# Attention scores of two heads at once, as 64-row fp32 products, in place of 128-row products of high and low parts

## The chip, the cores and the metric

The kernel runs on one core of one Trainium2 chip. The metric is the device time of one execution in microseconds (us); lower is better. The time before is 2332.83 us, the median of three runs (2322.44 to 2334.62).

## What is computed

The input is `[2, 2048, 256]` in fp32. A layer norm without gain is followed by causal attention with 16 heads of 64, a residual sum, a second layer norm, three blocks of quantised linear layers with GELU, and another residual sum. The part that matters here is the attention:

```python
keys    = einsum('bse,neh->bsnh', residual, W_key) + Bias_key       # S = 2048, 16 heads of 64
queries = einsum('bse,neh->bsnh', residual, W_query) + Bias_query
values  = einsum('bse,neh->bsnh', residual, W_values) + Bias_values
scores  = einsum('bknh,bqnh->bnqk', keys, queries) / sqrt(64)
scores  = where(q_idx < k_idx, 1e-10, scores)     # masked scores are 1e-10, not minus infinity
probs   = softmax(scores, axis=3)
weighted = einsum('bnqk,bknh->bqnh', probs, values)
```

A masked key still has a weight in the softmax, so the kernel adds a masked part to each numerator and denominator, and it needs the true maximum of each row before the exponentials.

## The kernel before, in words

Heads are worked on in pairs: 8 pairs per batch and 2 batches make N = 16 pairs. The 2048 queries of a pair are 4 groups of 512 columns, and its keys are 16 blocks of 128. `tiles_of` (line 38) cuts a group into tiles of two key blocks; there are NT = 20 tiles for each pair, in groups 3, 2, 1, 0. That makes 40 blocks per pair; 16 of them lie on the diagonal and have 512, 384, 256 or 128 columns, and the other 24 have 512.

TensorE's order is written out by hand (lines 932 to 945). While it works on tile t of pair i, it issues the score products of tile t+1 (`scores`, line 848), then the products with the values for tile t (`weighted`, line 869). Between them stand small pieces of the next pair's work, each at a slot number of a table, six slots to a tile: 12 projections (`project`, line 738, slots 0, 3, ..., 33), 40 pairs of bf16 products for the row maxima (`max_unit`, line 793, always at odd slots, table `MAX_AT`), transposes and denominators (`FIN`). ScalarE and VectorE follow the same tables.

The scores are done in TensorE's fast fp32r format, which is not exact to fp32. So every query and key is split in two. ScalarE writes the high part (`high`, line 955), VectorE writes what is left, the low part (`low`, line 1103), and both go to a tensor in device memory, `high_and_low` (`keep_split`, line 414). From there `install` (line 422) loads them as stacks of 128 rows: `kk` holds the key's high part twice, `qq` the query's high over its low part, `kl` the key's low part over a row of ones, `qm` the query's high part over the negated row maximum. One block of one head is then two products of 128 rows, L859 and L861, plus a bf16 product with `never_above` on the diagonal (L864). For two heads that is four products, and two more on the diagonal.

PSUM has 8 banks: 3 for scores (`SCORE_BANKS`), 4 that all background pieces take in turn (`BANKS`), and 1 for the outputs. A background piece waits in `bank_read` until the piece that had its bank BANKS places earlier has been read: a projection of queries or keys by VectorE's low part (`proj_read`), a max product by VectorE's maximum (`take_max`, L1118 or L1121).

The output side of a product with the probabilities uses 64 columns of the array for each head, so the two heads of L880 are two column tiles. The two heads of L798 are two row tiles of 64 rows each. All other products use the whole array.

Of the kernel before, what the change touches and what calls it, by code (L numbers as in the profile page):

```python
# [7 lines left out]
F32 = mybir.dt.float32  # L8
# [109 lines left out]
BANKS = 4  # L118
# [4 lines left out]
SCORE_BANKS = 3  # L123
# [12 lines left out]
def half_index(i, t, h, half):  # L136

    return NHALF * i + HALVES_TO[t] + len(halves_of(t)) * h + half
# [15 lines left out]
def background(n_pairs_in_all, n_pairs):  # L154
# [23 lines left out]
    counts = {"proj": 0, "max": 0, "fin": 0, "den": 0, "ln": len(PROJ_CHUNKS), "lora": 0, "weight": 0}  # L178
    for use in order:
        kind = {"vt": "fin", "mt": "fin"}.get(use[0], use[0])  # L180
        first[use] = len(users)
        for _ in range(2 if kind in ("max", "ln") else 1):
            counts[kind] += 1
            users.append((kind, counts[kind]))
# [8 lines left out]
def attention(nc, x, w_qkv, b_qkv, ffn_weights, parts, max_kept, kept, inverses, ot, home):  # L193
# [14 lines left out]
    with ExitStack() as ctx:  # L208
# [5 lines left out]
        def sem(name):  # L214
# [5 lines left out]
        never_above = sb("never_above", [P, P], BF16)  # L220
# [9 lines left out]
        split = [sb(f"split{b}", [P, 4, CH], F32R) for b in range(2)]  # L230
# [17 lines left out]
        qq = sb("qq", [P, 2, S], F32R)  # L248
        qm = sb("qm", [P, 2, S], F32R)
        kk = sb("kk", [P, 2, S], F32R)  # L250
        kl = sb("kl", [P, 2, S], F32R)
# [15 lines left out]
        w_q = ([split[0][:, l].bitcast(I32).rearrange("p (h d) -> p h d", h=halves) for l in range(4)]  # L267
               + [split[1][:, l].bitcast(I32).rearrange("p (h d) -> p h d", h=halves) for l in range(2)])
        w_unit = [t.bitcast(F32) for t in w_q]
        la_in = [xs[0:R, 3, l // 2, (l % 2) * D:(l % 2 + 1) * D] for l in range(4)]  # L270
        la_in += [split[1][0:R, 2, l * D:(l + 1) * D].bitcast(F32) for l in range(2)]
        lbt = [split[1][0:R, 3, l * D:(l + 1) * D].bitcast(F32) for l in range(2)]
# [17 lines left out]
        kl_zeroed = sem("kl_zeroed")  # L290
# [18 lines left out]
        proj_read = sem("proj_read")  # L309
# [4 lines left out]
        split_kept = [sem(f"split_kept{b}") for b in range(2)]  # L314
        stack_in = [sem(f"stack_in{c}") for c in range(4)]
# [59 lines left out]
        with nc.Block() as block:  # L375

            @block.sync
            def _(sp):
                def load_weights(j):

                    sp.wait_ge(proj_read, START + NPROJ * j)
# [15 lines left out]
                def load_ffn_weights():  # L397

                    sp.wait_ge(proj_done, START + NPROJ * N)
                    sp.wait_ge(bf_ready, START + 8 * N)  # L400
                    for b in range(2):
                        sp.wait_ge(split_kept[b], START + 64 * N)
                    for b, of in enumerate((slice(0, 4), slice(4, n_layers))):
                        n_of = of.stop - of.start
                        sp.dma_start(split[b][:, 0:n_of].bitcast(I32).rearrange("p l (h d) -> p (l h) d", h=halves),
# [3 lines left out]
                    sp.dma_start(split[1][0:R, 2].bitcast(F32).rearrange("r (l d) -> r l d", d=D),  # L409
# [3 lines left out]

                def keep_split(j, c):

                    k = PROJ_CHUNKS.index(c)
                    sp.wait_ge(proj_read, START + NPROJ * j + 3 * k + 2)
                    for h in range(2):
                        sp.dma_start(parts[j % 2, c].rearrange("z p h t -> h p z t")[h],
                                     split[k % 2][64 * h:64 * h + 64, :, :].bitcast(F32)).then_inc(split_kept[k % 2], 16)  # L420

                def install(j, c):

                    k = PROJ_CHUNKS.index(c)
                    sp.wait_ge(split_kept[k % 2], START + 64 * j + 32 * (k // 2 + 1))
                    of = parts[j % 2, c]
                    for dst, src in ((qq[:, :, cols(c)], of[0:2].rearrange("z p h t -> (z p) h t")),
                                     (kk[0:64, :, cols(c)], of[2]), (kk[64:128, :, cols(c)], of[2]),
                                     (qm[0:64, :, cols(c)], of[0]), (kl[0:64, :, cols(c)], of[3])):
                        sp.dma_start(dst.bitcast(F32), src).then_inc(stack_in[c], 16)  # L430
# [6 lines left out]
                def install_max(j, c):  # L437

                    sp.wait_ge(row_kept, START + 16 * (nth(j, c) + 1))
                    sp.dma_start(qm[64:65, :, cols(c)].bitcast(F32),  # L440
                                 max_kept[j % 2, c].rearrange("(o h r) t -> o h (r t)", o=1, h=2)).then_inc(row_in[c], 16)

                def install_chunk(j, c):

                    sp.wait_ge(pv_done, START + NT * (j - 1) + LAST_TILE[c] + 1)
                    install(j, c)
# [65 lines left out]
                for c in PROJ_CHUNKS:  # L512
                    keep_split(0, c)
                sp.wait_ge(consts, START + 1)
                load_weights(1)
                for c in GROUPS:
                    install(0, c)
# [5 lines left out]
                for i in range(N):  # L523
                    more = i + 1 < N
                    if i:
                        spread_inverse(i - 1, 1)
                        install_chunk(i, 0)
                        take_den(i - 1, 0)
                        install_max(i, 0)
                    if more:  # L530
                        keep_split(i + 1, 3)
                    if i:
# [6 lines left out]
                    if more:  # L539
                        keep_split(i + 1, 2)  # L540
                    spread_masked(i, 2)
                    if more:
                        keep_split(i + 1, 1)
# [1192 lines left out]
```

## Time and profile before

| | us |
|---|---|
| median of the runs before | 2332.83 |
| profiled execution, its own time | 2334.97 |
| span of its core | 2333.2 |
| TensorE busy | 2228.3 (96%) |
| VectorE busy | 1328.3 (57%) |
| ScalarE busy | 910.7 (39%) |
| GpSimd busy | 1350.7 (58%) |
| mean granted TensorE clock | 0.98 of full speed |

The attention fills the span up to about 2040 us; its first 94 us prepare the first pair. The feed-forward part follows. Every fp32 matmul appears as two records of TensorE, a product in fp32r or bf16 as one. An end of a matmul is modelled in the profile, so the time from one start to the next says more than the duration.

### The profile page before, as it was taken

Reading aid. Unit: us, or ns where it says so; the run is one execution under the profiler, and the core shown is the slowest. Engines: PE = TensorE matmul, PEld = TensorE weight load, DVE = VectorE, ACT = ScalarE, POOL = GpSimd, SP = SyncE. Lnnn points to the kernel's source line nnn. Section 1 sums busy time; section 2 is a strip of 40 time slices with the busy share of each in tenths; the row PEclk is TensorE's granted clock in tenths of the full one; section 3 lists DMA queues with packets and bytes.
Section 4 is the critical chain, followed back from the end, with each engine's and each line's share of the span. In section 5 each row is a group of like instructions: output and inputs, shape, how many; then the busy total and the mean of one; then the engine's idle time right before and its main releaser. Section 6 shows DMA issues by size and latency. Waiting matters only on the chain. (4 is left out here: it accounts for less than half of the span.)

```text
span 2333.2 us, 31181 instructions
## 1 busy us (share of the span) xinstructions
PE 2228.3 (96%) x10080; PEld 1133.2 (49%) x10080; DVE 1328.3 (57%) x3583; ACT 910.7 (39%) x1764; POOL 1350.7 (58%) x1211
## 2 busy tenths in 40 slices
PE   6899999999999999999999999999999998899987
PEld 2344444444444445444444444444444445777764
DVE  6755555555555566555656565555555563466664
ACT  2244444444444446444444444444444442110110
POOL 2277777777777777777677776767777611211110
PEclk9699999999999999999999999999999998999998
DMA  4644445454445463535363636363627323411100
GB/s 110 144 98 123 122 115 130 118 126 119 126 112 132 114 166 104 141 96 148 84 160 93 152 87 157 79 163 77 169 76 184 89 78 110 166 68 46 64 18 18
DMA packets 206272, 261.33 MB, mean 112 GB/s; under 512 B 74720, under 2 KB 91296, under 8 KB 206112
## 3 DMA queue, kind: packets, MB, share of 16 engines
q1 hardware_dynamic: 206112, 259.35, 42.2%
q8 instruction: 82, 1.34, 0.3%
q14 instruction: 78, 0.64, 0.1%
HBM read 169.87 MB, written 88.87 MB: 111 GB/s over the span
## 5 line engine op out<-in xcount | busy, mean ns | idle before, releaser
L711 POOL TENSOR_TENSOR acc<-acc,probs 128x512 f32<-128x512 f32 (+1 forms) x900 | 996.5, 1140 | 286.6 <-ACT probs L1056 286.4
L1056 ACT ACTIVATE probs<-ps_s 128x512 f32<-128x512 f32 (+1 forms) x1152 | 603.6, 576 | 740.1 <-PE ps_s L861 456.3
L1121 DVE TENSOR_REDUCE partial<-ps_bg 128x1 f32<-128x512 f32 x768 | 489.6, 684 | 201.2 <-PE ps_bg L798 200.2
L859 PE MATMUL ps_s<-qq,kk 128*128 128x512 f32 (+3 forms) x1280 | 579.5, 453 | 8.0 <-ACT probs L1056 4.9
L880 PE MATMUL ps_o<-probs,v 128*64 128x512 f32 (+3 forms) x2560 | 541.2, 543 | 1.8 <-DVE num L1145 1.8
L861 PE MATMUL ps_s<-qm,kl 128*128 128x512 f32 (+3 forms) x1280 | 469.4, 367 | 0.0
L746 PE MATMUL ps_bg<-home,w_in 128*128 128x512 f32 x768 | 368.6, 603 | 12.6 <-DVE split L1103 10.3
L859 PEld LDWEIGHTS ps_s<-qq,kk 128*128 128x128 f32 x1280 | 244.0, 191 | 202.2 <-issue 140.8
L798 PE MATMUL ps_bg<-k_bf,q_bf 64*128 64x512 bf16 (+3 forms) x1280 | 252.8, 363 | 21.2 <-DVE split L1103 14.0
L880 PEld LDWEIGHTS ps_o<-probs,v 128*64 128x64 f32 x2560 | 155.7, 136 | 233.4 <-issue 185.7
L861 PEld LDWEIGHTS ps_s<-qm,kl 128*128 128x128 f32 x1280 | 243.4, 190 | 37.4 <-issue 21.5
L1118 DVE CUSTOM_DVE_ANT_0 junk<-ps_bg,mask_q 128x512 bf16<-128x512 f32 (+3 forms) x512 | 229.0, 484 | 57.1 <-issue 55.1
L798 PEld LDWEIGHTS ps_bg<-k_bf,q_bf 64*128 64x128 bf16 x1280 | 67.2, 93 | 345.7 <-issue 283.4
L1103 DVE SCALAR_TENSOR_TENSOR split<-ps_bg,bias,split 128x512 fp32r<-128x512 f32 x128 | 94.3, 736 | 211.0 <-ACT q_bf L967 126.3
L746 PEld LDWEIGHTS ps_bg<-home,w_in 128*128 128x128 f32 x768 | 141.1, 191 | 119.9 <-issue 96.8
L1450 POOL TENSOR_TENSOR c_rstd<-c_var,c_minus_half 128x4 f32<-128x4 f32 x32 | 35.3, 1104 | 275.0 <-DVE c_var L1625 275.0
L704 POOL TENSOR_TENSOR acc<-probs 128x512 f32<-128x512 f32 x90 | 112.9, 1277 | 114.6 <-ACT probs L1056 67.3
L675 POOL TENSOR_TENSOR num<-num,scale 128x512 f32<-128x512 f32 x64 | 89.8, 1403 | 129.9 <-DMA scale<-inverse_sums 129.9
L964 ACT ACTIVATE split<-ps_bg,bias 128x512 fp32r<-128x512 f32 x128 | 88.0, 688 | 163.0 <-PE ps_bg L746 163.0
L1160 DVE RECIPROCAL inverse<-den_sq 32x32 f32<-32x32 f32 x64 | 21.5, 337 | 212.0 <-DMA den_sq<-den_rows 212.0
L667 POOL TENSOR_TENSOR masked_num<-v_from,e 128x512 f32<-128x512 f32 x64 | 76.9, 1201 | 89.7 <-DVE num L1145 88.5
L1598 ACT ACTIVATE c_yt<-c_ps,c_be,c_ga 128x512 f32<-128x512 f32 x48 | 33.7, 776 | 238.0 <-PE c_ps L1495 238.0
(114 smaller groups left out, 1886.4 us busy)
## 6 DMA issues: line engine op xcount, KB each, us to landing
high_and_low<-split SPq DMA_DIRECT2D x128, 512.0 KB, 5.9
qq<-high_and_low SPq DMA_DIRECT2D x64, 512.0 KB, 4.4
kk<-high_and_low SPq DMA_DIRECT2D x128, 256.0 KB, 5.3
qm<-high_and_low SPq DMA_DIRECT2D x64, 256.0 KB, 6.0
kl<-high_and_low SPq DMA_DIRECT2D x64, 256.0 KB, 6.3
e<-masked_weights SPq DMA_DIRECT2D x128, 128.0 KB, 3.0
scale<-inverse_sums SPq DMA_DIRECT2D x128, 128.0 KB, 2.9
heads_turned<-num SPq DMA_DIRECT2D x64, 256.0 KB, 3.3
```

The source lines that it names most:

```text
L675: g.tensor_tensor(num[:, n % NUMS, :], num[:, n % NUMS, :], scale[:, group % 2, :], ALU.mult).then_inc(o_ready, 1)
L704: g.tensor_tensor(acc[h][:, group % 2, :], pr[:, 0:CH], pr[:, CH:2 * CH], ALU.add).then_inc(added, 1)
L711: g.tensor_tensor(acc[h][:, group % 2, q0:q0 + w], acc[h][:, group % 2, q0:q0 + w], probs[h][:, probs_slot(i, t), at:at + w], ALU.add).the ...
L746: mm = pe.matmul(bank("proj", j, u), w_in[:, s, m, :], xs[:, c, s, :], start=(s == 0), stop=(s == halves - 1))
L798: pe.matmul(bank("max", j, n, h)[:, 0:w], q_bf[HEAD[h], qb * P:(qb + 1) * P], k_bf[HEAD[h], CH * u:CH * u + w], start=True, stop=True).the ...
L859: pe.matmul(out, kk[:, h, kb * P:(kb + 1) * P], qq[:, h, q], start=True, stop=False, skip_group_check=True)
L861: mm = pe.matmul(out, kl[:, h, kb * P:(kb + 1) * P], qm[:, h, q], start=False, stop=not diagonal, skip_group_check=True)
L880: mm = pe.matmul(ps_o[64 * h:64 * h + 64, q0:q0 + w], v[:, kb, 64 * h:64 * h + 64], probs[h][:, probs_slot(i, t), at:at + w], start=first, ...
L1056: nc.scalar.activation(probs[h][:, probs_slot(i, t), CH * half:end], ps_s[:, k % SCORE_BANKS, 0:end - CH * half], ACT.Exp, scale=SCORE_SCA ...
L1103: e.scalar_tensor_tensor(part[:, 2 * m + 1, :], bank("proj", j, u), bias[:, m:m + 1], part[:, 2 * m, :].bitcast(F32), ALU.add, ALU.subtrac ...
L1118: e.tensor_tensor_reduce(junk[:, k, 0:w], of, mask_q[:, CH - w:CH], 1.0, 3 * NEVER, ALU.add, ALU.max, to).then_inc(max_read, 1)
L1121: e.reduce_max(to, of, AX.X).then_inc(max_read, 1)
```

## The change

Queries and keys stay whole. ScalarE writes them in fp32 to `q_all` and `k_all`, both double-buffered by pair. One block of one head is one true fp32 product of 64 rows; the two heads lie in the upper and lower half of the array. A second product, of 64 rows in fp32r, adds the negated maximum of the row (`max_rows`, times one row of ones in `max_gate`). On the diagonal two bf16 products of 64 columns per head add the mask. VectorE's low part, the trips through `high_and_low` and the installs are gone; the row maximum is installed by two DMAs instead of one. A tile's four score calls become two, each for both heads, and the pieces that stood between them stand two by two. The scores get 4 banks and the background gets 3. A projection's bank is now free once ScalarE has read it.

```diff
-BANKS = 4
+BANKS = 3
-SCORE_BANKS = 3
+SCORE_BANKS = 4
...
-                    nc.scalar.activation(split[k % 2][:, 2 * m, :], bank("proj", j, u), ACT.Identity,
+                    exact = (q_all, k_all)[m]
+                    nc.scalar.activation(exact[:, j % 2, cols(c)], bank("proj", j, u), ACT.Identity,
...
-                    dve.wait_ge(hi_ready, START + 8 * j + 2 * (u // 3) + m + 1)
-                    dve.wait_ge(bf_ready, START + 8 * j + 2 * (u // 3) + m + 1)
-                    part = split[u // 3 % 2]
-                    e.scalar_tensor_tensor(part[:, 2 * m + 1, :], bank("proj", j, u), bias[:, m:m + 1],
-                                           part[:, 2 * m, :].bitcast(F32), ALU.add, ALU.subtract
-                                           ).then_inc(proj_read, 1)
...
-                    pe.matmul(out, kk[:, h, kb * P:(kb + 1) * P], qq[:, h, q], start=True, stop=False,
-                              skip_group_check=True)
-                    mm = pe.matmul(out, kl[:, h, kb * P:(kb + 1) * P], qm[:, h, q], start=False,
-                                   stop=not diagonal, skip_group_check=True)
+                    out = []
+                    for h in range(2):
+                        k = half_index(i, t, h, at // CH)
+                        if n == blocks[0] and k >= SCORE_BANKS:
+                            pe.wait_ge(p_ready, START + k - SCORE_BANKS + 1)
+                        out.append(ps_s[:, k % SCORE_BANKS, at % CH:at % CH + w])
+                        pe.matmul(out[h], k_all[HEAD[h], i % 2, kb * P:(kb + 1) * P], q_all[HEAD[h], i % 2, q],
+                                  start=True, stop=False, skip_group_check=True)
+                    last = [pe.matmul(out[h], max_gate[HEAD[h], :], max_rows[HEAD[h], q], start=False,
+                                      stop=not diagonal, skip_group_check=True) for h in range(2)]
                     if diagonal:
-                        mm = pe.matmul(bank_s[:, at % CH:at % CH + P], ident_bf[:, :], never_above[:, :], start=False,
-                                       stop=True, skip_group_check=True)
+                        for part in range(2):
+                            last = [pe.matmul(out[h][:, 64 * part:64 * part + 64], never_later[HEAD[h], h, part, :],
+                                              ident_bf[HEAD[h], 64 * h:64 * h + 64], start=False, stop=(part == 1),
+                                              skip_group_check=True) for h in range(2)]
...
-                        for h in range(2):
+                        if ni < N:
+                            scores_wait(ni, nt)
+                        for n in range(2):
                             if ni < N:
-                                scores_wait(ni, nt, h)
-                            for n in range(2):
-                                if ni < N:
-                                    scores(ni, nt, h, n)
-                                between(i, 6 * t + 2 * h + n)
+                                scores(ni, nt, n)
+                            between(i, 6 * t + 2 * n)
+                            between(i, 6 * t + 2 * n + 1)
```

## Rows read from the trace of the kernel before

**Rows 1.** Page, part 1: busy time, share of the span, instructions.
```profile
PE 2228.3 (96%) x10080; PEld 1133.2 (49%) x10080; DVE 1328.3 (57%) x3583; ACT 910.7 (39%) x1764; POOL 1350.7 (58%) x1211
```
**Rows 2.** Windows: stretch, length, busy time (instructions) by engine, clock, DMA share, GB/s.
```profile
0.00:94.00 94.00, 63.92 (x179) 22.97 (x180) 72.17 (x228) 20.04 (x35) 13.76 (x22) 0.81 0.59 143
236.00:1900.00 1664.00, 1634.49 (x7544) 760.32 (x7543) 947.44 (x2566) 756.61 (x1492) 1176.57 (x1054) 1.00 0.48 122
```
**Rows 3.** Waits of TensorE, whole span: total us, times, longest.
```profile
PE ps_bg L798 <- DVE split L1103: 14.0, 15, 0.9
PE ps_bg L746 <- DVE split L1103: 10.3, 8, 1.9
...
PE ps_s L859 <- ACT probs L1056: 4.9, 1, 4.9
```
**Rows 4.** Groups by form, TensorE: line, shapes, count, busy us, mean ns, idle before.
```profile
L859 PE MATMUL ps_s<-qq,kk 128*128 128x512 f32 x896 | 428.1, 478 | 8.0 <-ACT probs L1056 4.9 <-DMA qm<-maxima 3.1
...
L864 PE MATMUL ps_s<-never_above,ident_bf 128*128 128x128 bf16 x512 | 117.6, 230 | 0.0
```
**Rows 5.** Timeline, TensorE, 614.4 to 618.4 us: start, duration, instruction, records.
```profile
614.41 0.40 PE L861 MATMUL ps_s<-qm,kl 128*128 128x512 f32 x1
...
614.74 0.39 PE L798 MATMUL ps_bg<-k_bf,q_bf 64*128 64x512 bf16 x2
...
615.06 0.50 PE L859 MATMUL ps_s<-qq,kk 128*128 128x512 f32 x1
...
615.40 0.40 PE L861 MATMUL ps_s<-qm,kl 128*128 128x512 f32 x1
...
615.64 0.40 PE L859 MATMUL ps_s<-qq,kk 128*128 128x512 f32 x1
...
615.88 0.40 PE L861 MATMUL ps_s<-qm,kl 128*128 128x512 f32 x1
...
616.21 0.39 PE L798 MATMUL ps_bg<-k_bf,q_bf 64*128 64x512 bf16 x2
...
616.52 1.94 PE L880 MATMUL ps_o<-probs,v 128*64 128x512 f32 x8
...
618.39 0.39 PE L798 MATMUL ps_bg<-k_bf,q_bf 64*128 64x512 bf16 x2
```
**Rows 6.** Timeline, TensorE, 609.3 to 611.1 us: a projection and what follows.
```profile
609.29 1.88 PE L746 MATMUL ps_bg<-home,w_in 128*128 128x512 f32 x4
...
611.10 0.39 PE L798 MATMUL ps_bg<-k_bf,q_bf 64*128 64x512 bf16 x2
```
**Rows 7.** Timeline, TensorE, 646.0 to 646.4 us: a diagonal block of 256 columns.
```profile
645.97 0.39 PE L859 MATMUL ps_s<-qq,kk 128*128 128x256 f32 x1
646.19 0.28 PE L861 MATMUL ps_s<-qm,kl 128*128 128x256 f32 x1
646.31 0.23 PE L864 MATMUL ps_s<-never_above,ident_bf 128*128 128x128 bf16 x1
646.35 0.31 PE L859 MATMUL ps_s<-qq,kk 128*128 128x128 f32 x1
```
**Rows 8.** Groups of VectorE from 236 to 1900 us, columns as in rows 4.
```profile
L1121 DVE TENSOR_REDUCE partial<-ps_bg 128x1 f32<-128x512 f32 x672 | 429.6, 685 | 187.0 <-PE ps_bg L798 186.1
...
L1134 DVE TENSOR_TENSOR_SCAN v_from<-ones_row,v_from,vt 128x512 f32<-128x512 bf16 x56 | 86.8, 1550 | 1.5
L1103 DVE SCALAR_TENSOR_TENSOR split<-ps_bg,bias,split 128x512 fp32r<-128x512 f32 x109 | 80.1, 735 | 172.2 <-ACT q_bf L967 99.9 <-ACT k_bf L967 72.1
L1097 DVE TENSOR_SCALAR vt<-ps_bg,bias 128x512 f32<-128x512 f32 x55 | 41.3, 751 | 39.2 <-PE ps_bg L746 39.2
L1152 DVE TENSOR_TENSOR den_rows<-ps_bg,den_rows 65x512 f32<-65x512 f32 x56 | 38.4, 686 | 60.2 <-PE ps_bg L825 30.6 <-DMA den_rows<-masked_den 29.5
```
**Rows 9.** Timeline, all engines, 91.7 to 93.7 us: the end of the preparation.
```profile
91.70 0.67 SPq L440 DMA_DIRECT2D qm<-maxima  x1
...
93.68 0.77 PE L859 MATMUL ps_s<-qq,kk 128*128 128x512 f32 x1 [3.08 <-DMA qm<-maxima]
```

More of the change, by code:

```diff
@@ L136, in half_index @@
 def half_index(i, t, h, half):
-    return NHALF * i + HALVES_TO[t] + len(halves_of(t)) * h + half
+    return NHALF * i + HALVES_TO[t] + 2 * half + h
 def tile_end(i, t):
@@ L190, with attention @@
 NFIRST = len(FIN_FIRST)
-def attention(nc, x, w_qkv, b_qkv, ffn_weights, parts, max_kept, kept, inverses, ot, home):
+def attention(nc, x, w_qkv, b_qkv, ffn_weights, max_kept, kept, inverses, ot, home):
     n_chunks, _, _, D = x.shape
@@ L229, in attention @@
         xs = home.rearrange("p (c s t) -> p c s t", c=4, s=halves)
-        split = [sb(f"split{b}", [P, 4, CH], F32R) for b in range(2)]
+        staged = [sb(f"staged{b}", [P, 4, CH]) for b in range(2)]
         vt = sb("vt", [P, S])
@@ L556, in _ @@
                     masked_rows(i, 3)
-                    if more:
-                        install_chunk(i + 1, 3)
                     take_den(i, 3)
@@ L621, in _ @@
                 g.memset(minus_half[:, :], -0.5).then_inc(zeroed, 1)
-                for tile in (ident, ident_bf, never_above, mask_q):
+                for tile in (ident, ident_bf, mask_q):
                     g.memset(tile[:, :], 0.0).then_inc(zeroed, 1)
+                g.memset(never_later[:, :, :, :], 0.0).then_inc(zeroed, 1)
                 pool.wait_ge(zeroed, START + 5)
@@ L650, in _ @@
                 pool.wait_ge(set_up, START + 1)
-                g.memset(kl[64:65, :, :].bitcast(F32), 1.0).then_inc(consts, 1)
+                for h in range(2):
+                    g.memset(max_gate[64 * h:64 * h + 1, :].bitcast(F32), 1.0).then_inc(consts, 1)
                 def masked_denominators(i):
@@ L925, in _ @@
                             turn_values(0, c)
-                pe.wait_ge(consts, START + 1)
-                for h in range(2):
-                    scores_wait(0, 0, h)
-                    for n in range(2):
-                        scores(0, 0, h, n)
+                pe.wait_ge(consts, START + 2)
+                scores_wait(0, 0)
+                for n in range(2):
+                    scores(0, 0, n)
                 turn_max(0, 0)
@@ L1033, in _, with exponentials @@
                         high(0, n)
-                act.wait_ge(consts, START + 1)
+                act.wait_ge(consts, START + 2)
                 for k, (kind, c) in enumerate(FIN_FIRST[:-1]):
                     evacuate(0, kind, c, k + 1)
-                def exponentials(i, t, h, n):
+                def exponentials(i, t, n):
                     tile = TILES[t][1]
-                    if h == 0 and n == 0:
+                    half = tile[n][3] // CH
+                    if n != halves_of(t)[half][-1]:
+                        return
+                    if half == 0:
                         user = NT * i + t - NP_SLOTS
@@ L1049, in exponentials @@
                                 act.wait_ge(fin_written, START + fin_before(i, 0))
-                    half = tile[n][3] // CH
-                    if n != halves_of(t)[half][-1]:
-                        return
-                    k = half_index(i, t, h, half)
                     end = tile[n][3] + tile[n][2]
-                    act.wait_ge(s_ready, START + k + 1)
-                    nc.scalar.activation(probs[h][:, probs_slot(i, t), CH * half:end],
-                                         ps_s[:, k % SCORE_BANKS, 0:end - CH * half], ACT.Exp,
-                                         scale=SCORE_SCALE).then_inc(p_ready, 1)
-                for h in range(2):
-                    for n in range(2):
-                        exponentials(0, 0, h, n)
+                    for h in range(2):
+                        k = half_index(i, t, h, half)
+                        act.wait_ge(s_ready, START + k + 1)
+                        nc.scalar.activation(probs[h][:, probs_slot(i, t), CH * half:end],
+                                             ps_s[:, k % SCORE_BANKS, 0:end - CH * half], ACT.Exp,
+                                             scale=SCORE_SCALE).then_inc(p_ready, 1)
+                for n in range(2):
+                    exponentials(0, 0, n)
                 evacuate(0, "mt", 0, NFIRST)
@@ L1066, in _ @@
                         t = n // 6 + 1
[L1067 to L1070 removed]
+                        if n % 6 in (0, 2) and t < NT:
+                            exponentials(i, t, n % 6 // 2)
+                        elif n % 6 in (0, 2) and i + 1 < N:
+                            exponentials(i + 1, 0, n % 6 // 2)
                         for u in range(NPROJ):
```

139 lines of the change are left out of this document (45 added, 94 removed).

## The prediction

> **What bounds the kernel now.** I read the busy times first. TensorE is busy for 96% of the span, every other engine for under 60% [rows 1]. The windows then say where: from 236 to 1900 us, which is nearly all of the attention, TensorE is busy 1634.49 of 1664 us at full clock, while GpSimd, the next, has 1176.57 and ScalarE 756.61 [rows 2]. The list of its waits confirms that it is hardly ever held up: 14.0 and 10.3 us for VectorE's low parts, 4.9 us for an exponential [rows 3]. So in the attention the time is the length of TensorE's own list, and what another engine saves is worth nothing unless TensorE waited for it. Only the first 94 us differ: there VectorE is busy for 72.17 us, TensorE for 63.92 with its clock at 0.81 [rows 2]. The feed-forward part isn't touched.
>
> Durations of matmuls overlap, so I price them by the distance from one start to the next. Two fp32r products of 512 columns start 0.24 us apart (615.40, 615.64, 615.88) [rows 5]. An fp32 product on the whole array costs 0.86: two of them take from 609.29 to 611.10, 1.81 us, about 0.10 of which is the change to what follows [rows 6]. Four fp32 products on column tiles of 64 take from 616.52 to 618.39, 1.87 us for two pairs [rows 5]: less such a change 0.86 to 0.90 a pair, so the two heads overlap fully.
>
> **The change part by part.**
>
> *A, blocks off the diagonal.* There are 896 products of 512 columns at L859, and 512 products on the diagonal, a quarter of which are 512 wide [rows 4]: 896 - 128 = 768, or 384 blocks of two heads. Before, such a block is four fp32r products, 4 x 0.24 = 0.94 us (they are 0.233 to 0.24 apart). After, it is one row pair in fp32 and one row pair in fp32r. No row shows an fp32 row pair. From below it can't be quicker than one fp32 product, 0.86; from above it is two of them, 1.72. I take 0.86, since the fp32 column pair [rows 5] and the bf16 row pair (0.32 with its change, both heads together) both overlap. The fp32r pair is 0.24, at most 0.48. So 0.86 + 0.24 = 1.10 against 0.94: +0.16 x 384 = **+61 us**.
>
> *B, the 256 diagonal blocks.* One head's block of 256 columns costs 0.38 us, from 645.97 to 646.35 [rows 7], two heads 0.76. After: the fp32 pair 0.43 (half of 0.86), the fp32r pair 0.12 to 0.24, and two pairs of masks of 64 columns. Their price is not shown; the nearest row is the mask of 128 columns before, 0.04 to its successor (646.31 to 646.35) [rows 7], so 0.08 to 0.20 for both pairs. The sum is 0.63 to 0.87, -0.13 to +0.11 per block, and as a 512-wide block gains A's 0.16 on top, up to +0.3. I take +0.02: **+5 us**, with -33 and +77 as its ends.
>
> *C, changes between array layouts.* A max pair stands in the 64-row layout. 614.41 to 614.74 is 0.33 where 0.24 is normal; the pair itself takes 0.32; the first score product after it 0.34 [rows 5]. Entering, leaving and starting again cost some 0.10 each. I counted the order by the slot tables. Before, a pair of heads has 93 changes of layout, 27 of them into a score product, which pays twice: 93 x 0.10 + 27 x 0.10 = 12.0 us. After, scores and maxima share the layout, so the 22 changes from a max pair to a score and 18 back are gone, but projections and transposes, which shared the scores' layout, now need them: 82 changes, 11 into scores, 9.3 us, plus 17 starts of projections and transposes at 0 to 0.10, say 0.05: 10.2. The difference is 1.8 to 2.0 us in each of 15 pairs: **-30 us**; ends 0 and -90 (below).
> The Trainium skill ("TensorEngine Tiling (Array Packing)", Key Properties) says that changing the tiling mode drains TensorE, while changing the tile does not. The trace agrees: the extra 0.09 to 0.10 stands at the changes alone. By a reading of it in which only the 40 changes at maxima counted, C would be -60 us; by its letter the new ones at projections count as well, which is what I took.
>
> *D, waits that go.* The low parts held TensorE for 14.0 + 10.3 us [rows 3]. They are gone and the bank of a projection is free after ScalarE, which the low part waited for anyway: **-24 us**, ends -24 and -10.
>
> *E, three background banks instead of four.* This is the added wait. The second product of a max pair now takes the bank of the first product of the max pair before it, which must have been read; behind it on TensorE's queue stand all further scores and value products. That read ends about 0.39 + 0.68 + 0.10 = 1.2 us after its product starts (0.39 [rows 5], 0.685 [rows 8]; 0.10 for two handovers is my allowance). Where the value products lie between, max pairs are 2.2 us apart (616.21 to 618.39), with 1.0 to spare; where scores lie between they were 1.47 apart (614.74 to 616.21) [rows 5] and will be 0.22 + 1.10 = 1.3. The slack is 0.1 us. What VectorE does besides then comes out: 4 scans, 4 value projections and 4 denominators per pair, 4 x (1.55 + 0.75 + 0.69) = 12.0 us [rows 8]. 22 of 40 max pairs are followed by a score, so 6.6 us per pair could show, 99 us in all; 0 is the other end. The nearest row is the wait that a bank more left: 24 us, all behind low parts of 0.735 us, 8 per pair [rows 3, 8]. I take **+25 us**.
>
> *F, the first 94 us.* VectorE loses 8 low parts of 0.735, 5.9 us [rows 8], and the first score no longer waits 3.08 us for its row of maxima [rows 9], which was queued behind the installs. TensorE's last maxima are late next, and they follow VectorE: **-7 us**, ends 0 and -12.
>
> *At nothing:* 512 fewer transfers: TensorE waited for a DMA once in the attention [rows 9]. ScalarE's two passes over each projection stay. The order of exponentials changes, but ScalarE has 756.61 of 1664 us [rows 2] and four score banks in place of three. GpSimd's sums are unchanged. The second DMA for each row of maxima is behind a full tile of work.
>
> Sum: 61 + 5 - 30 - 24 + 25 - 7 = +30 us. The profiled execution took 2334.97 us, so 2365; it is 2.1 above the median of the runs, so I predict **2363 us**, with its own range from 2335 to 2400.
>
> **The rivals.**
> 1. *It cancels.* VectorE keeps ahead, E is 0: 2338 us. For it: it waits 187.0 us for maxima before L1121 [rows 8], so it is early on the whole. Against: the short distances above. Chance 0.15.
> 2. *Faster: the layout changes decide.* At 22 x 0.20 + 18 x 0.09 = 6.0 us per pair, 90 us in all go, if the new changes at projections cost nothing because the two row tiles run out one after the other while the next weights load; E is 5. 61 + 5 - 90 - 24 + 5 - 7 = -50: 2283 us. It decides once the saving passes 60 us, 4 us per pair. Against: projection to max pair costs the change just the same (609.29 to 611.10) [rows 6]. Chance 0.10.
> 3. *VectorE becomes the bound through the banks.* E is 99: 2437 us. Chance 0.10.
> 4. *The fp32r row pair does not hide.* It streams 0.24 us, in which weights for both heads must come in, now four times per block instead of two; one after the other it is 0.48: 0.24 x 384 + 0.12 x 256 = +123: 2486 us. Weight loads are 0.11 us each on the mean (1133.2 over 10080) [rows 1], which two at once just fit. Chance 0.05.
> The Trainium skill ("TensorE: Matmul & The Clock Gate", LDWEIGHTS) says that a load's time goes by its columns and not by its rows, so a 64-row load is as long as a 128-row one. That speaks for this rival; no 64-row fp32 load is in this trace.
> 5. *The fp32 row pair does not overlap at all.* +0.86 x 384 + 0.43 x 256 = +440: about 2800 us. Against it stand both kinds of pair in rows 5. Chance 0.03.
>
> **How the numbers follow.** The forecast has 0.57. Within 0.5% means 2321 to 2344 us, about what a measurement of this kernel can tell from no change. Faster: rival 2 and an edge of the forecast, 0.12. Same: rival 1 and the forecast's lower edge, 0.21. Slower: the rest, 0.67. The range is 2318 to 2440: it leaves out rival 2, rivals 4 and 5.
>
> **What the profile of the changed kernel would show.** A: starts of the fp32 row products 0.43 us apart with both heads at one time, a 512-wide block 1.10 us in all; 1.3 or more refutes it. B: diagonal blocks of 256 at 0.63 to 0.87. C: max pair to score 0.22, and 0.10 extra around each projection. D: no wait of TensorE behind a projection of queries or keys. E: TensorE's waits for L1118, L1121, L1134 or L1152 add up to 25 us, most of them where scores stand between max pairs. F: the first score at about 87 us instead of 93.68. The prediction is wrong if the clock of the attention falls below 1.00, if row pairs don't overlap, or if E is far from 25.

## The result, and the profile of the changed kernel

The changed kernel takes 2340.87 us in the median of 15 runs, the kernel before 2327.24 in as many (its first three, known at the forecast, had 2332.83). The ratio on record is 1.0075, with an interval from 1.0061 to 1.0088: slower by 14 to 20 us; the two medians alone are 13.6 us apart. One of the 15 runs of the changed kernel, 2586.83 us at a granted clock of 0.842, is left out of the ratio. The way was forecast, the size was not: 2363 us, 30 us above the median known then. Of the 22 us between 2363 and 2340.87, some 6 come from that median, which the later runs lowered, and 16 from the change itself.

The first view is the page of the changed kernel: busy times, and what the DMA queues moved.

```profile
PE 2251.2 (96%) x11872; PEld 1024.5 (44%) x11872; DVE 1233.5 (53%) x3455; ACT 904.0 (39%) x1764; POOL 1346.7 (58%) x1212
...
DMA packets 117192, 93.71 MB, mean 40 GB/s; under 512 B 67552, under 2 KB 84128, under 8 KB 117024
```

TensorE is still the bound and 23 us busier than in [rows 1]. VectorE has lost 95 us of work, and the DMAs have shrunk from 261.33 MB to 93.71. The windows (columns as in [rows 2]) show the attention at full clock, and TensorE idle for 16 us of 1664, where it was 29.5:

```profile
236.00:1900.00 1664.00, 1647.87 (x9106) 661.38 (x9102) 866.41 (x2452) 749.09 (x1488) 1178.56 (x1054) 1.00 0.12 34
```

Next, TensorE's timeline in the changed kernel: start, duration, instruction, records. A max pair, a block, another block, a max pair, the value products:

```profile
622.29 0.39 PE L759 MATMUL ps_bg<-k_bf,q_bf 64*128 64x512 bf16 x2
622.52 1.02 PE L817 MATMUL ps_s<-q_all,k_all 64*128 64x512 f32 x4
622.97 0.80 PE L819 MATMUL ps_s<-max_rows,max_gate 64*128 64x512 f32 x2
623.61 1.02 PE L817 MATMUL ps_s<-q_all,k_all 64*128 64x512 f32 x4
624.06 0.79 PE L819 MATMUL ps_s<-max_rows,max_gate 64*128 64x512 f32 x2
624.70 0.39 PE L759 MATMUL ps_bg<-k_bf,q_bf 64*128 64x512 bf16 x2
625.02 1.94 PE L841 MATMUL ps_o<-probs,v 128*64 128x512 f32 x8
```

Block to block is 1.09 us (622.52 to 623.61). The four records of the two fp32 heads all start within 0.43 us; the two that belong together start 3 to 4 ns apart, so both heads take 0.86 us and the maximum's pair the other 0.23. A max pair before a score costs 0.23 (622.29 to 622.52) where it cost 0.32 in [rows 5]; before the value products it still costs 0.32.

Spans alone say little here, so the comparison goes pair by pair. I took the start of the first value product of each pair of heads, and the distance to the next pair's. "Last pair" is from its first value product to its last, "rest" what comes behind:

```
                        first value   15 distances      clean pair   last pair   rest
                        product       together
before                  104.48        1759.94           116.1         79.2       389.6
changed                 101.71        1773.59           118.0         73.0       390.8
difference               -2.8          +13.7             +1.9          -6.2       +1.2   = +5.9
```

A clean pair is the commonest distance. In the changed kernel twelve of 15 pairs take 117.98 to 118.06 us; the others are 119.0, 124.1 (the one with the second batch's layer norm) and 114.1 (the last distance). In the kernel before only four take 116.1; nine are uneven, 116.3 to 119.8, the one with the layer norm takes 120.3 and the last 114.6. So the clean pair grew by 1.9 us, 29 us in all, and 15 us of unevenness and 6 us of the last pair went. (The two profiled executions are 5.9 us apart and the medians 13.6, since the profiled one of before, 2334.97, is 7.7 above its median. That the unevenness differs from run to run would explain this; it isn't shown, since one execution of each kernel is profiled.)

Where the last pair of before lost its time stands in four views of that kernel: the timelines of VectorE, the DMA queue, ScalarE and TensorE.

```profile
1879.91 0.34 DVE L1160 RECIPROCAL inverse<-den_sq 32x32 f32<-32x32 f32 x1 [8.41 <-DMA den_sq<-den_rows]
```
```profile
1869.17 0.57 SPq L430 DMA_DIRECT2D qq<-high_and_low  x1
1869.78 1.26 SPq L430 DMA_DIRECT2D kk<-high_and_low  x2
1871.08 0.60 SPq L430 DMA_DIRECT2D qm<-high_and_low  x1
1871.72 0.60 SPq L430 DMA_DIRECT2D kl<-high_and_low  x1
1872.45 1.21 SPq L483 DMA_DIRECT2D den_sq<-den_rows  x2
```
```profile
1882.42 1.58 ACT L1056 ACTIVATE probs<-ps_s 128x512 f32<-128x512 f32 x3 [5.96 <-DVE acc L1191]
```
```profile
1883.07 0.79 PE L859 MATMUL ps_s<-qq,kk 128*128 128x512 f32 x1 [4.90 <-ACT probs L1056]
1883.66 0.63 PE L861 MATMUL ps_s<-qm,kl 128*128 128x512 f32 x1
1884.22 3.68 PE L880 MATMUL ps_o<-probs,v 128*64 128x512 f32 x8
1887.83 0.53 PE L859 MATMUL ps_s<-qq,kk 128*128 128x512 f32 x1
```

The sums of the denominators, a tiny transfer, are issued behind the five installs of chunk 0, and VectorE goes on 7.4 us after that (1872.45 to 1879.91). VectorE stands in its reciprocal for 8.41 us; in the last pair it also adds the probabilities, so ScalarE waits 5.96 us for VectorE, and TensorE 4.90 us for ScalarE. Then TensorE works at the lower level of its clock (1.2 GHz) until 1887.9: value products that take 1.94 elsewhere take 3.68. The same lower level stands in two other pairs of that trace, for 3.41 us from 1410.1 and from 1529.5, behind waits of 1.75 and 1.90 us for a low part at L746; they are the two longest of the uneven ones, 119.65 and 119.79 us.

TensorE's waits in the changed kernel, the whole span (the feed-forward part's left out):

```profile
PE ps_bg L759 <- ACT k_bf L924: 7.3, 15, 0.5
...
PE ps_bg L759 <- DVE den_rows L1102: 4.2, 14, 1.2
PE ps_bg L707 <- ACT k_bf L924: 3.2, 3, 1.1
...
PE ps_bg L759 <- DVE partial L1068: 2.4, 6, 1.0
PE ps_bg L759 <- DVE partial L1071: 1.5, 5, 0.3
```

With six smaller ones these are 24.5 us, all for a background bank. This isn't to be set against the 24.3 for low parts in [rows 3] alone: the kernel before waited about 8 us more for such banks, of which these are the larger two:

```profile
PE ps_bg L798 <- DVE partial L1118: 3.6, 9, 1.6
...
PE ps_bg L798 <- DVE partial L1121: 1.6, 5, 0.4
```

### The profile page after: what moved, and what is told of

The parts are those of the page before. It is cut to its first block and busy times, and to the rows that moved or that the text cites. A ratio compares the mean times of both kernels' runs of the same rounds, so it can differ in the third digit from the quotient of the medians.

```text
span 2339.1 us, 33962 instructions
## 1 busy us (share of the span) xinstructions
PE 2251.2 (96%) x11872; PEld 1024.5 (44%) x11872; DVE 1233.5 (53%) x3455; ACT 904.0 (39%) x1764; POOL 1346.7 (58%) x1212
## 2 busy tenths in 40 slices
DMA packets 117192, 93.71 MB, mean 40 GB/s; under 512 B 67552, under 2 KB 84128, under 8 KB 117024
## 5 line engine op out<-in xcount | busy, mean ns | idle before, releaser
L1014 ACT ACTIVATE probs<-ps_s 128x512 f32<-128x512 f32 (+1 forms) x1152 | 588.6, 572 | 754.3 <-PE ps_s L819 491.8
L817 PE MATMUL ps_s<-q_all,k_all 64*128 64x512 f32 (+3 forms) x2560 | 609.7, 549 | 0.0
L819 PE MATMUL ps_s<-max_rows,max_gate 64*128 64x512 f32 (+3 forms) x1280 | 453.5, 696 | 0.0
L707 PE MATMUL ps_bg<-home,w_in 128*128 128x512 f32 x768 | 381.8, 620 | 6.9 <-ACT k_bf L924 3.2
L759 PE MATMUL ps_bg<-k_bf,q_bf 64*128 64x512 bf16 (+3 forms) x1280 | 269.3, 361 | 19.7 <-ACT k_bf L924 7.3
L817 PEld LDWEIGHTS ps_s<-q_all,k_all 64*128 64x128 f32 x2560 | 223.7, 188 | 126.8 <-ACT probs L1014 66.9
L1055 DVE TENSOR_SCALAR vt<-ps_bg,bias 128x512 f32<-128x512 f32 x64 | 48.1, 751 | 305.0 <-PE ps_bg L707 305.0
L819 PEld LDWEIGHTS ps_s<-max_rows,max_gate 64*128 64x128 f32 x1280 | 128.3, 187 | 114.8 <-issue 104.9
L628 POOL TENSOR_TENSOR masked_num<-v_from,e 128x512 f32<-128x512 f32 x64 | 76.1, 1190 | 89.6 <-DVE num L1095 88.3
L1102 DVE TENSOR_TENSOR den_rows<-ps_bg,den_rows 65x512 f32<-65x512 f32 x64 | 44.0, 687 | 94.7 <-PE ps_bg L786 45.9
L1469 PE MATMUL c_ps<-c_yt,home 128*128 128x512 f32 x192 | 86.8, 605 | 4.9 <-ACT c_yt L1548 4.9
```

The costliest lines, as they stand in the source:

```text
L707: mm = pe.matmul(bank("proj", j, u), w_in[:, s, m, :], xs[:, c, s, :], start=(s == 0), stop=(s == halves - 1))
L759: pe.matmul(bank("max", j, n, h)[:, 0:w], q_bf[HEAD[h], qb * P:(qb + 1) * P], k_bf[HEAD[h], CH * u:CH * u + w], start=True, stop=True).the ...
L817: pe.matmul(out[h], k_all[HEAD[h], i % 2, kb * P:(kb + 1) * P], q_all[HEAD[h], i % 2, q], start=True, stop=False, skip_group_check=True)
L819: last = [pe.matmul(out[h], max_gate[HEAD[h], :], max_rows[HEAD[h], q], start=False, stop=not diagonal, skip_group_check=True) for h in ra ...
L1014: nc.scalar.activation(probs[h][:, probs_slot(i, t), CH * half:end], ps_s[:, k % SCORE_BANKS, 0:end - CH * half], ACT.Exp, scale=SCORE_SCA ...
L1469: mm = pe.matmul(ps[L][:, s, :], w[:, 2 * k + 1, r, s * P:(s + 1) * P], yt[L][:, r, :], start=(r == 0), stop=(r == halves - 1))
```

## The experiments

Each ran on one chip beside the kernel before; ratios are against that. All diffs are against the kernel named first.

**1. The projections moved (changed kernel).**
```diff
-PROJ_SLOT = [3 * u for u in range(NPROJ)]
+PROJ_SLOT = [6 * (u // 2) + 3 + 2 * (u % 2) for u in range(NPROJ)]
+MAX_AT = [n - 1 if n % 6 == 3 else n for n in MAX_AT]
```


> The changed kernel with the next pair's projections at slots 3 and 5 of each six (beside the value products) instead of 0 and 3, and the max pairs of slot 3 one slot earlier. Theory (each change between array layouts costs about 0.10 us, and 0.10 more where fp32 or fp32r work starts): 66 changes per pair of heads instead of 82, and 5 fewer starts of scores after a projection, so about 2.1 us less in each of 15 pairs, 32 us less than the changed kernel, ratio to the kernel before about 0.992. Rival (the layout changes cost nothing, the clean pair of 118.0 us is longer for another reason): same time as the changed kernel, ratio 1.0075. Second rival (moved work collides with the three background banks): slower than 1.0075.

Measured: 2315.17 us, 0.9962 (0.9949 to 0.9976). Its clean pair takes 116.3 us instead of 118.0, its 15 distances 1748.84 us: 24.8 less. A clean pair gives 0.08 us for each of the 21 changes and starts, near the 0.10 of the theory, and both rivals are out. This kernel already beats both.

**2. The same move in the kernel before.**
```diff
-PROJ_SLOT = [3 * u for u in range(NPROJ)]
+PROJ_SLOT = [6 * (u // 2) + 3 + 2 * (u % 2) for u in range(NPROJ)]
```


> The kernel before with the projections at slots 3 and 5, nothing else. Here projections share the scores' layout, so the move buys nothing: 98 changes instead of 93, 5 x 0.10 x 15 = 8 us slower, ratio 1.003. If moving projections helped for a reason that has nothing to do with layouts (banks, ScalarE's order), this kernel would gain as well: 0.99.

Measured: 2347.21 us, 1.0106 (1.0088 to 1.0125). There it costs 25 us, three times what was expected; so experiment 1's gain is not one of moving as such. The clean pair is 116.8 us instead of 116.1, where the theory's five more changes were to cost 0.5. The rest is unevenness: TensorE waits 14.2 us for VectorE's value projection in that kernel, a wait that the original didn't show.

**3. Scores in fp32r (changed kernel).** The edit gives `q_all` and `k_all` the type fp32r.
```diff
-        q_all = sb("q_all", [P, 2, S])
-        k_all = sb("k_all", [P, 2, S])
+        q_all = sb("q_all", [P, 2, S], F32R)
+        k_all = sb("k_all", [P, 2, S], F32R)
```


> The changed kernel with the 64-row score product in fp32r instead of fp32 (the scores lose the exactness of fp32). Theory (A): a pair of 512 columns costs 0.24 instead of 0.86 us, so 384 x 0.62 = 238 us and on the 256 diagonal blocks about 0.3 each, 77 us: 315 us less if TensorE stays the bound, about 2026 us, ratio 0.870. Rival (ScalarE, GpSimd or VectorE takes over at once): GpSimd is busy 1346.7 us of 1180 to 1900 in the attention; it would hold the time at about 2150 us or more, ratio 0.92.

Measured: 2244.42 us, 0.9661 (0.9643 to 0.9679): a third of the 315 us. TensorE's waits say why (236 to 1900 us):

```profile
PE ps_bg L759 <- DVE partial L1068: 104.8, 44, 7.0
PE ps_bg L759 <- DVE partial L1071: 10.0, 29, 0.4
```

GpSimd, the rival's bound, is busy for 1185.21 of these 1664 us and isn't it. With quick scores TensorE is held by VectorE, and a clean pair is 112.5 us, with 10.7 us of idle TensorE where the changed kernel had 1.0. Most of that is one stop, which comes back in nearly every pair. Here it is in VectorE's and TensorE's timelines:

```profile
621.62 8.79 DVE L1084 TENSOR_TENSOR_SCAN v_from<-ones_row,v_from,vt 128x512 f32<-128x512 bf16 x1
```
```profile
630.81 0.28 PE L759 MATMUL ps_bg<-k_bf,q_bf 64*128 64x128 bf16 x1 [6.93 <-DVE partial L1068]
```

One scan of VectorE takes 8.79 us, 14 times in this run; in the changed kernel 47 of 64 take 1.3 us and none over 2.2. The maxima behind it are late, TensorE stops for 6.9 us, and its granted clock is at the lower level (1.2 GHz) for 10.24 us, from 626.6 to 636.8, so the 6 us of work behind the stop go at half speed. Why the scan is so long there no run shows. The last pair, which has no such stop, is 17.4 us shorter (55.6 against 73.0), close to the 315 / 16 = 19.7 us of the theory. So the fp32 price is real, but most of it is lost again to this stop and the slow clock behind it.

**4. Four background and three score banks (changed kernel).**
```diff
-BANKS = 3
+BANKS = 4
-SCORE_BANKS = 4
+SCORE_BANKS = 3
```


> The changed kernel with four background banks and three score banks, as before the change. Theory (E): the fourth bank takes back TensorE's waits in the attention for a background bank, 11.7 us for ScalarE and 11.6 us for VectorE in the list of waits, and three score banks cost nothing: 20 us less, ratio 0.999. Rival: both heads' scores are issued together, so with three score banks the second block must wait for an exponential of the first: more than 1.0075.

Measured: 2447.74 us, 1.0536 (1.0517 to 1.0555). The rival was right. The clean pair is 125.1 us. The waits of TensorE's weight loads in the window 236 to 1900 us, first of this kernel, then of the changed one, show 75 us more of waiting for an exponential:

```profile
PEld ps_s L817 <- ACT probs L1014: 129.8, 199, 0.8
```
```profile
PEld ps_s L817 <- ACT probs L1014: 54.8, 73, 0.8
```

One thing got faster: with four background banks the first score starts at 81.07 us, in the changed kernel at 89.67.

**5. The kernel before without installs from pair 1 on.** `install_chunk` keeps its wait and issues nothing; the score products wait for pair 0's installs alone.
```diff
-                    install(j, c)
...
-                            pe.wait_ge(stack_in[c], START + 80 * (i + 1))
+                            pe.wait_ge(stack_in[c], START + 80)
```


> The kernel before with the install DMAs of pairs 1 to 15 left out (their scores use pair 0's queries and keys; the row maxima are still installed). Theory (transfers cost time where a denominator's small transfer is queued behind an install): in the last pair VectorE waited 8.41 us for den_sq, TensorE then 4.90 us for an exponential and went on at half clock; that stall goes, 9 us less, and the uneven pairs (116.1 to 120 us each) get closer to 116.1: ratio 0.992 to 0.996. Rival (installs are hidden, as the prediction had it at nothing): 1.000, and a last pair of 79 us as before.

Measured: 2310.68 us, 0.9936 (0.9922 to 0.9950). Thirteen of the 15 distances are 116.1 to 116.3 us, and the last pair takes 71.9 instead of 79.2. The installs were not hidden. In its trace the pairs are 25 us shorter together, though the first value product comes 4.6 us later.

**6. The sums ahead of the installs (kernel before).** Two lines change places; all work stays.
```diff
-                        install_chunk(i, 0)
                         take_den(i - 1, 0)
+                        install_chunk(i, 0)
```


> The kernel before with one line moved: the denominators' transfer of the last group is issued ahead of the installs of chunk 0 instead of behind them. Nothing is left out. Theory: the last pair takes about 71 to 73 us instead of 79.18, the rest stays: 7 us less, ratio 0.997. Rival (the 7.4 us of the small transfer are not due to the installs ahead of it): 1.000.

Measured: 2311.10 us, 0.9940 (0.9925 to 0.9954), twice the expected gain. The last pair is 71.9 us and the clean ones are 116.1, as if the installs weren't there: the rival is out. VectorE's waits, first before, then here:

```profile
DVE inverse L1160 <- DMA den_sq<-den_rows: 212.0, 31, 8.8
```
```profile
DVE inverse L1160 <- DMA den_sq<-den_rows: 102.8, 22, 7.4
```

TensorE's list of waits no longer has the 10.3 us at L746 of [rows 3] nor the 4.9 for an exponential; the other wait for low parts is the same to the digit:

```profile
PE ps_bg L798 <- DVE split L1103: 14.0, 15, 0.9
```

So 10.3 of the 24.3 us "for low parts" were the installs' doing. The trace is 24.6 us shorter in its pairs (17.3 in the 15 distances, 7.3 in the last), the median 14 us. VectorE still waits 102.8 us for sums, but TensorE isn't held up by that.

**7. A short low part (kernel before).** From pair 1 on it has 8 columns.
```diff
-                    e.scalar_tensor_tensor(part[:, 2 * m + 1, :], bank("proj", j, u), bias[:, m:m + 1],
+                    lw = slice(0, CH if j == 0 else 8)
+                    e.scalar_tensor_tensor(part[:, 2 * m + 1, lw], bank("proj", j, u)[:, lw], bias[:, m:m + 1],
...
```


> The kernel before with VectorE's low part of 8 columns instead of 512 from pair 1 on (the rest of the low parts is left as it was, so the scores of those pairs are wrong in their low bits); its waits for ScalarE stay. Theory (D): TensorE's 24 us of waits for low parts shrink by the 0.7 us that each takes: 15 us less, ratio 0.993. Rival (VectorE's length does not matter, only its wait for ScalarE): 1.000.

Measured: 2311.48 us, 0.9937 (0.9921 to 0.9954). Its profiled execution took 7710.27 us, so its trace isn't read. The gain is as expected, but 6 gives as much, so it doesn't say by itself whether both are one stall.

**8. Both (6 and 7).**

> before_sums_first with the low part of 8 columns from pair 1 on (low bits of the scores are left as they were). Theory (with the installs out of the way the low parts hold TensorE only 0.9 us in each pair): another 0.9 x 15 = 13 us less at most, ratio 0.989. Rival (both earlier gains of 14 us were the same stall, and a VectorE that is on time hides its low parts): 0.994 again.

Measured: 2301.05 us, 0.9889 (0.9874 to 0.9905): 0.5% below experiment 6, 10 to 12 us. They are two things. The trace shows less than the times: a clean pair is 115.5 us instead of 116.1, and TensorE's wait at L798 falls from 14.0 to 6.1 us. So the low part costs TensorE some 0.6 us per pair even when VectorE is on time.

**9. The changed kernel's order, in the kernel before.** The loops over heads and blocks change places in `scores` and `exponentials`, `half_index` becomes `2 * half + h`, and the background pieces stand two by two.
```diff
-    return NHALF * i + HALVES_TO[t] + len(halves_of(t)) * h + half
+    return NHALF * i + HALVES_TO[t] + 2 * half + h
...
-                        for h in range(2):
+                        if ni < N:
+                            scores_wait(ni, nt, 0)
+                        for n in range(2):
...
-                            for n in range(2):
-                                if ni < N:
+                                for h in range(2):
...
+                            between(i, 6 * t + 2 * n)
+                            between(i, 6 * t + 2 * n + 1)
```


> The kernel before with the block order of the changed kernel: both heads of a block together, exponentials likewise, background pieces two by two; the products, layouts and banks stay. Theory (order alone costs nothing, the 2 us per pair come from products and layouts): 1.000. Rival (issuing both heads together needs the fourth score bank, as 107 us for taking it away from the changed kernel suggest): up to 100 us more, ratio 1.02 to 1.045.

Measured: 2315.06 us, 0.9957 (0.9941 to 0.9972). Neither theory: the order gains 10 us, and its last pair is still 78.2 us long, so this isn't the installs' stall. The clean pair is 115.6 instead of 116.1; by the slot tables the order has 90 changes of layout instead of 93 and 24 starts of scores instead of 27, six items for 0.5 us. And three score banks are enough here, so the 107 us of 4 come with the order only when the fp32 products are in it.

**10. Order and sums first together (kernel before).**

> The kernel before with the block order of the changed kernel and the denominators' transfer ahead of the installs. If the two add up (115.6 us for a clean pair, 71.9 for the last): 8 us less than before_sums_first, about 2303 us, ratio 0.991. Rival (the order's gain of 0.0043 was the same waits for low parts): 0.994.

Measured: 2304.69 us, 0.9893 (0.9872 to 0.9914). They add up: the clean pair is 115.6 us and the last 71.3.

**11. Three background and four score banks (kernel before).**
```diff
-BANKS = 4
+BANKS = 3
...
-SCORE_BANKS = 3
+SCORE_BANKS = 4
```


> The kernel before with three background banks and four score banks. Theory (E as forecast, the low part is read last): TensorE waits for VectorE's low parts and maxima through the missing bank, some 25 to 60 us more, ratio 1.01 to 1.025. Rival (the score banks are worth more than the background bank, as in the changed kernel, where the fourth score bank was worth 107 us): under 1.00.

Measured: 2392.47 us, 1.0269 (1.0243 to 1.0294), just above the expected range:

```profile
PE ps_bg L746 <- DVE split L1103: 36.3, 19, 3.2
...
PE ps_bg L798 <- DVE split L1103: 20.1, 15, 1.3
```

The waits for low parts are 56.4 us where they were 24.3, a further 10 us are lost before the first value product, and TensorE's clock is at the lower level in seven places for 3.41 us each. A low part that is read last lives badly with three banks; ScalarE's reading does better (24.5 us of waits in all in the changed kernel). Each kernel is slower with the other's bank counts.

**12. The masks left out (changed kernel).**
```diff
-                    diagonal = kb // 4 == group
+                    diagonal = False
```


> The changed kernel without the bf16 mask products on the diagonal (the causal mask of those blocks is left out of the scores). Theory (from the starts in its trace: a 512-wide diagonal block 1.165 us, an off-diagonal one 1.09, so two mask pairs cost 0.07): 256 x 0.07 = 18 us less, ratio to the kernel before about 1.000. Rival (masks cost what the forecast allowed at most, 0.20): 51 us less, 0.986.

Measured: 2322.29 us, 0.9984 (0.9970 to 0.9998): 0.9% or 19 to 21 us under the changed kernel, 0.07 to 0.08 for each of 256 blocks. As read from the starts.

**13. Fewer changes (on 1).** Transposes and denominators go beside the value products too.
```diff
-FIN = [("vt", 0, 3), ("vt", 3, 50), ("den", 3, 60), ("mt", 3, 72), ("vt", 2, 86), ("mt", 2, 96), ("den", 2, 98),
-       ("den", 1, 110), ("vt", 1, 113), ("mt", 1, 114), ("mt", 0, 119), ("den", 0, SLOTS)]
+FIN = [("vt", 0, 3), ("vt", 3, 50), ("den", 3, 62), ("mt", 3, 69), ("vt", 2, 86), ("mt", 2, 93), ("den", 2, 98),
+       ("mt", 1, 105), ("den", 1, 110), ("vt", 1, 111), ("mt", 0, 117), ("den", 0, SLOTS)]
-INVERT_SLOT = {3: 68, 2: 106, 1: 118, 0: SLOTS + 8}
+INVERT_SLOT = {3: 70, 2: 106, 1: 118, 0: SLOTS + 8}
```


> after_projections_moved with the transposes and the denominators also moved beside the value products. 60 changes of layout per pair instead of 66 and 3 fewer starts of fp32 work: 9 x 0.10 x 15 = 13 us less than after_projections_moved, ratio 0.990. Rival (the transposes now stand where VectorE's maxima are late): no gain, 0.996 or above.

Measured: 2308.93 us, 0.9914 (0.9896 to 0.9932). Clean pair 115.9, 0.46 less than in 1: 0.05 us for each of nine changes and starts, half of the theory's 0.10. The 15 distances are together only 5.3 us shorter, where 13 were expected.

**14. Projections two by two (on 13).**
```diff
-PROJ_SLOT = [6 * (u // 2) + 3 + 2 * (u % 2) for u in range(NPROJ)]
+PROJ_SLOT = [6 * (u // 2) + 3 for u in range(NPROJ)]
```


> after_fewer_changes with two projections at a time at slot 3 of each six, none at slot 5. 54 changes and 6 fewer starts: 12 x 0.10 x 15 = 18 us less than after_fewer_changes at most, ratio 0.983. Rival (three banks: the second projection needs the bank of the max product issued 1.1 us before it, and VectorE's read of it ends 1.2 us after its start): most of that comes back as waits, 0.988 to 0.996.

Measured: 2287.86 us, 0.9832 (0.9810 to 0.9855), the best of all. Clean pair 114.5, 1.37 less: 0.11 us for each of twelve. The rival's waits hardly came: TensorE's wait for L1069 behind L760 is 5.6 us here as in 13, and the only new one is 2.8 us at the projections.

## Why the prediction had the way right and the size wrong

**What bounds the kernel** was right: in both kernels the clean pair is TensorE's own list, in which it is idle for 0.93 us before and 1.0 after, and experiments 1, 13 and 14, which only reorder that list, all moved the time the way the count of changes says.

**A** was right. A block is 1.09 us, forecast 1.10; before, 0.94. 384 x 0.15 = +58 us, forecast +61. The fp32 row pair overlaps in full, and rival 4's weight loads hide: one of 64 rows at L817 takes 0.19 us, as one of 128 rows at L859 did.

**B** was too high. The forecast was +5. From start to start, the diagonal blocks of 512, 384, 256 and 128 columns of two heads take 1.17, 0.98, 0.62 and 0.46 us; before it was 1.16, 0.95, 0.77 and 0.63. These rows of the changed kernel show a block of 256: 0.72 us to the next, of which 0.10 is the change to the transpose, against 0.76 in [rows 7].

```profile
647.68 0.59 PE L817 MATMUL ps_s<-q_all,k_all 64*128 64x256 f32 x4
647.92 0.47 PE L819 MATMUL ps_s<-max_rows,max_gate 64*128 64x256 f32 x2
648.24 0.23 PE L823 MATMUL ps_s<-ident_bf,never_later 64*128 64x64 bf16 x4
648.40 0.38 PE L765 MATMUL ps_bg<-ident,neg_max 128*8 128x128 f32 x2
```

That is -0.28 for four blocks, -18 us in all. What the forecast missed stands in [rows 7]: the first product of a block, behind a bf16 mask, takes 0.22 us (645.97 to 646.19), the second 0.12. So before, each head's diagonal block paid about 0.09 us for its start, and a block of both heads paid twice; in the changed kernel both heads start together. The masks cost 0.07 to 0.08 (12), not up to 0.20.

**C** was too large. From the changed kernel to 14, 28 changes and 14 starts per pair went and the 15 distances fell from 1773.59 to 1721.28: 0.083 us each on the mean, not 0.10. It is a mean of unlike steps, 0.08, 0.05 and 0.11 in experiments 1, 13 and 14, so it isn't a fixed price. I took the starts of projections and transposes at half; counted in full, the change gave 93 + 27 against 82 + 28: 10 x 0.083 x 15 = -12 us (8 to 17), forecast -30. That each start pays in full is an assumption; no run separates starts from changes. The mechanism is the one named, and the reading by which only the changes at maxima count, -60 us, is out: changes at projections cost too.

**D and E** were forecast at +1 together. Their sum looks right by luck; neither part is. D: the 24.3 us went, but 10.3 of them were the installs' stall (6), so the low parts' own share was 14.0. And the forecast's sign for D, no wait of TensorE behind a projection of queries or keys, failed: 11.7 us are for ScalarE's reading of one. E: the added waits for VectorE's maxima, scans and sums of denominators are 11.6 us against 6.7 before, so +5 and not +25, "far from 25" by the forecast's own sign of being wrong. Without the stall, that is between experiment 6 and the changed kernel, TensorE's idle time in the pairs rose from 14.4 to 17.1 us: D and E together +3. The fourth score bank, which the forecast gives as a reason for pricing the new order at nothing, is worth 107 us in the changed kernel (4).

**F**: the first score starts 4.0 us earlier, at 89.67, the first value product 2.8 us, forecast 7. But not for the reasons given. TensorE's very first product already starts 3.4 us earlier, at 13.53 instead of 16.94, after a shorter clearing of memory that the forecast didn't name: VectorE's for `max_rows` takes 1.76 us, that for `qm` took 3.47 (that this is the cause isn't tested). The wait for the row of maxima (3.08) and VectorE's low parts went, yet from that first product to the first score it is 76.1 us against 76.7: the gain was lost to three banks, with four of them the first score starts 8.6 us sooner (4).

**The step that failed** is the one "at nothing: 512 fewer transfers: TensorE waited for a DMA once in the attention". It looked at TensorE's direct waits only. VectorE's wait for den_sq, 212.0 us in the list of waits, ends in TensorE's waits under other names: the 10.3 us of late low parts at L746 in [rows 3] and the 4.9 us "for an exponential", which I read and did not follow back. Experiments 5 and 6 put it at 14 us of the median and 24.6 of the profiled execution. This gain the change has, and the forecast left it out. Two terms of the sum were mis-sized as well: B at +5, which measured -18, and C at -30, which came to -12.

The sum with what was measured, against the profiled execution: A +58, B -18, C -12, D and E +3, F -3, the rest behind the last pair +1, the installs' stall -25 (17.3 us in the distances, 7.3 in the last pair): +4, and +5.9 were measured. The 2 us left over mean little, as C alone is known to some 5 us. Without the stall on either side, experiment 6 against the changed kernel, the change costs 1.0075 / 0.9940 = 1.014 or some 31 us, 32.2 between the two traces. That is near the forecast of 30, but by luck: B was 23 us too high and C 18 us too low, and D and E missed by about 10 and 20 us in opposite ways.

## What to carry to other kernels

A wait of the bounding engine is the end of a chain: follow each back to the first engine that waited for a transfer, before a DMA is priced at nothing; a small transfer that another engine stands still for belongs ahead of the large ones on its queue. Where TensorE works in several array layouts, count the changes between them from the order of issue, at some 0.08 us each here (0.05 to 0.11 by step), and put pieces of one layout together: that was worth 2% and turned the slower kernel into the fastest. Divide the banks anew for each order of issue: the fourth score bank was worth 107 us to the changed kernel, and in the kernel before the same order did without it.

## What the runs showed of the hardware that was not expected

Two fp32 products of 64 rows in different halves of the array run side by side as fully as bf16 ones: both in 0.86 us. One 4.9 us stop of TensorE was followed by 4.8 us of work at 1.2 GHz, so the last pair lost 7.3 us, one and a half times the stop's length. And a transfer of 2 x 2 KB (the sums) took 7.4 us behind five installs of 256 and 512 KB; the median over all such transfers in that trace is 2.5 us. A scan of 512 columns on VectorE took 8.79 us in 14 places of experiment 3's trace and 1.3 to 2.2 in its other 50, for a reason that stays open.
